# Cross attention with x1 turned and multiplied two pairs behind instead of three, w loaded and split earlier, the mask matmul of pair 0 last

## The chip, the cores and the metric

The kernel is one launch on one core of a Trainium2 chip. TensorE (PE) multiplies, VectorE (DVE), ScalarE (ACT) and GpSimd (POOL) do the elementwise work, SyncE (SP) and ACT issue the transfers. Each engine has its own stream of instructions and takes them in order; a semaphore holds an instruction until others have been counted. The metric is the device time of the launch in microseconds; smaller is better.

## The reference

Three blocks on x (32 sequences of 64 tokens, 512 wide), one after the other:

```
x = x + cross_attention(layernorm(x), ctx, mask)    # ctx: 32 x 256 x 512
x = x + latent_attention(layernorm(x), ...)         # 16 heads; q from 384, kv from 128 latent columns, rope on 64
x = x + ffn(layernorm(x), ...)                      # 512 -> 2048 -> 512, an expert term, a layernorm
```

Cross attention, with the latents that the next block needs, is what the change touches:

```
scores = einsum('bsd,bmd->bsm', hidden, memory) / sqrt(D);  scores = where(mask, scores, -1e30)
readout = einsum('bsm,bmd->bsd', softmax(scores), memory);  x1 = x + readout
q = rmsnorm(layernorm(x1) @ wq_a.T + b);  kv, k_pe = layernorm(x1) @ wkv_a.T + b   # kv normed, k_pe rotated
```

## The kernel before

`stage_x` handles the 2048 tokens as 16 pairs of sequences, 128 tokens each. Every engine runs `slot(p, par)` for p from 0 to 15; an order written out by hand in `slot` sets what stands behind what on each engine. In slot p the kernel works on several pairs at once:

- Pair p: `score(p)` on PE multiplies the turned, normalised x (`xnT0`) with the turned context (`ctxT`, ring of four) in eight matmuls (sixteen rows in the trace), onto the mask rows that a first matmul (`picks`) put there. DVE takes `maximum(p)`, ACT `exp(p)`, PE turns the probabilities into `b_prob`.
- Pair p+1: PE `turn0(p+1)` turns `xn0`; ACT `turned0(p+1)` copies it to `xnT0`.
- Pair p+2: DVE `first_var(p+2)` takes mean and variance; POOL `rstd_of(0, p+2)` makes rstd and shift; ACT `norm(0, ...)` applies them one slot later.
- Pair p-1: ACT `turned_probs` copies `b_prob` to `pT`; PE `read(p-1)` multiplies it with `ctx_in` (ring of four); DVE `residual(p-1)` adds it to x, which is x1, and takes its mean and variance; POOL `rstd_of(1, p-1)`, ACT `norm(1, ...)` to `xn1`.
- Pair p-2: PE `turn1` turns `xn1`, ACT `turned1_hi` copies it rounded, DVE `turned1_lo` takes the rest, so that three matmuls (hi and lo, `mm3`) make up a full one.
- Pair p-3: PE `project` multiplies it with the latent weights `w_hi`, `w_lo` (24 matmuls to `b_z`); DVE `bias` adds the bias to `zb`.
- Pair p-4: ACT `squares`, DVE `latent_var`, POOL `latent_rstd` and `rotate` (four steps), ACT `scale_q`, DVE `latent_kv`; `write_z` on ACT's queue stores the latents.

SP loads x, `ctxT`, `ctx_in`, and once `w_raw` (1152 KB) and `small`. `w_hi` is a cast of `w_raw`, `w_lo` a subtraction on DVE. After slot 15 the last pairs are drained by calls written out in `program`, between fills of the next block's weights (`fill_keys`, `keys_hi`, `keys_lo`, `fill_bias`; `rope_scaled` on POOL multiplies two blocks of 1536 columns). A reader should keep three waits in mind: `project(p)` waits for `xT1_lo`, `score(p)` for `xT0`, `norm(1, p)` for `shift1`.

Of the kernel before, what the change touches and what calls it, by code (L numbers as in the profile page):

```python
# [182 lines left out]
def stage_x(nc, ctx, A, scratch, mem, banks, w):  # L183
# [204 lines left out]
    def scalar(act):  # L388
# [42 lines left out]
        def slot(p, par):  # L431
# [4 lines left out]
            if has(p - 4):  # L436
                squares(p - 4, par)
            exp(p)
            if has(p - 4):
                scale_q(p - 4, par)  # L440
# [1672 lines left out]
```

## Time and profile before

| | us |
|---|---|
| Median of three runs (1086.8, 1087.6, 1095.32) | 1087.6 |
| Profiled execution, device time | 1087.94 |
| Its span, first to last instruction | 1086.1 |
| PE busy, share of the span | 1061.9, 98% |
| DVE, ACT, POOL busy | 509.6, 338.8, 295.5 |

The cross attention stage ends some 165 us into the span. A busy share tells how much an engine does, not whether it is waited for; the rows of the next sections are read for that. Starts and durations in a timeline are in microseconds from the span's start, an instruction's end may overlap the next one's start, and the bracket at a row's end says how long the engine was idle before it and who released it.

### The profile page before, as it was taken

What the parts mean: (1) busy time and instruction counts of PE and PEld (TensorE: products, weight loads), DVE (VectorE), ACT (ScalarE), POOL (GpSimd) and SP (SyncE); (2) the same over time, 40 slices, a digit from 0 to 9 for tenths busy, and PEclk for the clock granted to TensorE, in tenths of its full rate; (3) what the DMA queues carried; (4) which work ended last, traced back from release to release, by engine and by line L of the source; (5) the groups of instructions that cost most, each with busy time, mean ns of one, the idle gap of its engine ahead of it and who ended that gap; (6) DMA issues with size and microseconds to landing.
All of it is one profiled execution on the core that took longest, in us unless ns stands there. A gap on an engine that the chain in (4) does not pass through costs nothing.

```text
span 1086.1 us, 18670 instructions
## 1 busy us (share of the span) xinstructions
PE 1061.9 (98%) x7233; PEld 902.5 (83%) x7233; DVE 509.6 (47%) x914; ACT 338.8 (31%) x630; POOL 295.5 (27%) x341
## 2 busy tenths in 40 slices
PE   5999999999999999999999999999999999999997
PEld 3677787788888888888888889999999898989896
DVE  3666565545455554445545668532324241414232
ACT  3565554423222222222322236312222221313030
POOL 2434462311112101131113102423233232415050
PEclk9999999999999999999999999999999999999999
DMA  9999962200022000320012083200101010101000
GB/s 361 414 418 386 395 257 85 69 21 20 21 69 88 20 22 11 107 59 21 20 59 88 20 261 87 72 23 17 39 1 40 1 39 0 39 1 39 1 21 20
DMA packets 40851, 101.26 MB, mean 93 GB/s; under 512 B 7049, under 2 KB 11172, under 8 KB 36292
## 3 DMA queue, kind: packets, MB, share of 16 engines
q1 hardware_dynamic: 39044, 96.62, 25.0%
q10 hardware_dynamic: 1728, 3.54, 0.8%
q8 instruction: 55, 0.90, 0.3%
q14 instruction: 24, 0.20, 0.1%
HBM read 74.45 MB, written 17.30 MB: 84 GB/s over the span
## 4 chain that ended last, share of the span: by engine, by line
PE 94%; DVE 2%; issue 1%; DMA 1%; POOL 1%; ACT 0%; SPq 0%; POOLq 0%; DVEq 0%; ACTq 0%
PE b_z L44 6%; PE b_z L46 6%; PE b_z L45 6%; PE b_score L44 5%; PE b_score L46 5%; PE b_prob L46 5%; PE b_prob L44 5%; PE b_score L45 5%; PE b_prob L45 5%; PE b_turn L44 4%; PE b_turn L46 4%; PE b_turn L45 4%; PE b_read L46 4%; PE b_read L44 4%; PE b_read L45 4%; PE b_read L619 2%
## 5 line engine op out<-in xcount | busy, mean ns | idle before, releaser
L1501 POOL TENSOR_TENSOR f_hT_lo<-f_h,f_hT_hi 128x512 fp32r<-128x512 f32 x64 | 92.5, 1445 | 106.2 <-ACT f_hT_hi L1546 96.9
L810 POOL TENSOR_TENSOR m_sc<-m_sc,m_rs 128x1024 f32<-128x1024 f32 x16 | 30.6, 1910 | 241.8 <-DVE m_rs L973 241.8
L1602 DVE TENSOR_TENSOR f_h<-f_h 128x512 f32<-128x512 f32 x64 | 49.8, 777 | 91.7 <-ACT f_h L1541 91.7
L44 PE MATMUL b_z<-m_zT_lo,m_wq_hi 128*128 128x512 f32 x192 | 75.0, 390 | 0.9 <-issue 0.6
L46 PE MATMUL b_z<-m_zT_hi,m_wq_hi 128*128 128x512 f32 x192 | 74.7, 389 | 0.0
L45 PE MATMUL b_z<-m_zT_hi,m_wq_lo 128*128 128x512 f32 x192 | 74.7, 389 | 0.0
L44 PE MATMUL b_turn<-f_xnT_lo,f_up_hi 128*128 128x256 f32 x256 | 72.6, 283 | 0.1
L44 PE MATMUL b_read<-f_xnT_lo,f_up_hi 128*128 128x256 f32 x256 | 72.5, 283 | 0.0
L45 PE MATMUL b_read<-f_xnT_hi,f_up_lo 128*128 128x256 f32 x256 | 72.4, 283 | 0.0
L46 PE MATMUL b_turn<-f_xnT_hi,f_up_hi 128*128 128x256 f32 x256 | 72.4, 283 | 0.0
L45 PE MATMUL b_turn<-f_xnT_hi,f_up_lo 128*128 128x256 f32 x256 | 72.4, 283 | 0.0
L46 PE MATMUL b_read<-f_xnT_hi,f_up_hi 128*128 128x256 f32 x256 | 72.4, 283 | 0.0
L981 DVE TENSOR_TENSOR m_x<-b_score,m_x 128x512 f32<-128x512 f32 x32 | 22.1, 690 | 95.1 <-PE b_score L46 95.1
L852 ACT ACTIVATE m_qT<-b_z,m_q_bias 128x512 f32<-128x512 f32 x64 | 44.0, 689 | 70.4 <-PE b_z L46 64.6
L800 POOL TENSOR_TENSOR m_qpe<-m_qpe,m_swapped 128x512 f32<-128x512 f32 x32 | 41.4, 1292 | 79.0 <-DMA m_swapped<-m_by_sin 79.0
L1546 ACT CAST f_hT_hi<-f_h 128x512 fp32r<-128x512 f32 x64 | 39.8, 622 | 57.3 <-DVE f_h L1602 57.3
L1541 ACT ACTIVATE f_h<-b_turn 128x512 f32<-128x512 f32 x32 | 19.1, 598 | 112.8 <-PE b_turn L46 112.8
L1483 POOL TENSOR_TENSOR f_ve<-f_mv,m_eps 128x2 f32<-128x2 f32 x15 | 3.4, 227 | 182.3 <-DVE f_mv L1576 182.3
L873 ACT ACTIVATE m_sc<-m_sc 128x512 f32<-128x512 f32 x32 | 20.2, 632 | 104.8 <-DVE m_sc L965 104.8
L44 PE MATMUL b_score<-m_wvo_lo,m_oT_hi 128*128 128x512 f32 x128 | 51.4, 401 | 0.0
L44 PE MATMUL b_score<-f_down_lo,f_hT_hi 128*128 128x512 f32 x128 | 50.5, 394 | 0.3 <-issue 0.3
L44 PE MATMUL b_prob<-m_wvo_lo,m_oT_hi 128*128 128x512 f32 x128 | 50.6, 395 | 0.0
(268 smaller groups left out, 3098.6 us busy)
## 6 DMA issues: line engine op xcount, KB each, us to landing
x_ctx_in<-ctx_rows_dram SPq DMA_DIRECT2D x16, 1024.0 KB, 14.9
x_ctxT<-ctx_turned_dram SPq DMA_DIRECT2D x15, 1024.0 KB, 14.5
m_swapped<-m_by_sin SPq DMA_DIRECT2D x128, 64.0 KB, 2.0
m_raw<-attn_raw_dram SPq DMA_DIRECT2D x6, 768.0 KB, 10.9
m_z_in<-z_scratch SPq DMA_DIRECT2D x4, 1152.0 KB, 5.7
x_x_all<-x_dram SPq DMA_DIRECT2D x16, 256.0 KB, 15.1
m_x<-x_scratch SPq DMA_DIRECT2D x4, 1024.0 KB, 6.0
x_scratch<-m_x SPq DMA_DIRECT2D x4, 1024.0 KB, 5.1
```

Of the source, the lines that this page charges most:

```text
L44: nc.tensor.matmul(out, lh, rl, start=first, stop=False)
L45: nc.tensor.matmul(out, ll, rh, start=False, stop=False)
L46: return nc.tensor.matmul(out, lh, rh, start=False, stop=last)
L619: mm = t.matmul(b_read[rows], pT[:, c, rows], ctx_in[:, p % RING, chunks * b + c], start=c == 0, stop=c == chunks - 1)
L800: q.tensor_tensor(qpe[:, m], qpe[:, m], swapped[:], ALU.add).then_inc(s["qpe_done"], 1)
L810: q.tensor_tensor(e, e, rs[:].unsqueeze(2).broadcast_to([P, HB, SEQ]), ALU.mult).then_inc(s["normed"], 1)
L852: a.activation(qT[:, h], b_q[h % 2][:], ACT.Identity, bias=q_bias[:, HU * n + h:HU * n + h + 1]).then_inc(s["q_done"], 1)
L873: a.activation(sc[:, HALF * half:HALF * half + HALF], sc[:, HALF * half:HALF * half + HALF], ACT.Exp, scale=SCALE).then_inc(s["exped"], 1)
L981: v.tensor_tensor(x1[:, TILES[i]], b_w[i % 2][:], x1[:, TILES[i]], ALU.add).then_inc(s["x2_done"], 1)
L1501: g.tensor_tensor(hT_lo[:, 2 * n:2 * n + 2].rearrange("p m n -> p (m n)"), h[:, n % 2], hT_hi[:, 2 * n:2 * n + 2].bitcast(F32).rearrange(" ...
L1546: a.copy(hT_hi[:, 2 * n:2 * n + 2].rearrange("p m n -> p (m n)"), h[:, n % 2]).then_inc(s["h_hi"], 1)
L1602: v.tensor_tensor(h[:, n % 2], h[:, n % 2], h[:, n % 2], ALU.mult).then_inc(s["squared"], 1)
```

## The change

The order of the slots moves: on every engine the work that stood at p-3 (project, bias) is now at p-2 and that at p-4 at p-3. On TensorE, turn1(p-2) moves ahead of read(p-1), in slot 2 even ahead of score(2), with project(0) behind score(2). On ACT the hi copy moves ahead of exp, on DVE the lo copy ahead of first_var. The cast to `w_hi` moves from POOL in slot 2 to ACT in slot 1, ahead of norm(1, 0); w is loaded ahead of ctxT(2). 22 transposes of the identity precede turn0(0). The mask matmul of pair 0 comes last in its group. `rope_scaled` moves from behind slot 15 into slots 14 and 15, first on POOL. The drain in `program` is one pair shorter.

```
+    WARM = 22
 (sync)
+        load_ctxT(1)
         load_x(2)
-        load_ctxT(1)
         load_ctx(0)
         load_x(3)
+        sp.dma_start(w_raw[:], ...).then_inc(s["w_loaded"], 16)
         load_ctxT(2)
+        load_x(4)
         load_ctx(1)
-        load_x(4)
-        sp.dma_start(w_raw[:], ...).then_inc(s["w_loaded"], 16)
+        sp.dma_start(small[:], A["small"]).then_inc(s["small_loaded"], 16)
         load_ctxT(3)
 (gpsimd slot)
+            if p >= PAIRS - w.ROPE_ROUNDS:
+                rope_scaled(p - (PAIRS - w.ROPE_ROUNDS))
             if has(p + 2):
                 rstd_of(0, p + 2)
-            if has(p - 4):
-                latent_rstd(p - 4)
-                rotate(p - 4, par)
+            if has(p - 3):
+                latent_rstd(p - 3)
+                rotate(p - 3, 1 - par)
             if has(p - 1):
                 rstd_of(1, p - 1)
-            if p == 2:
-                pool.wait_ge(s["w_loaded"], 16)
-                g.tensor_copy(w_hi[:], w_raw[:]).then_inc(s["w_hi"], 1)
 (scalar slot)
+            if has(p - 3):
+                squares(p - 3, 1 - par)
             if has(p - 2):
                 turned1_hi(p - 2, par)
+            exp(p)
+            if has(p - 3):
+                scale_q(p - 3, 1 - par)
             if has(p + 1):
                 turned0(p + 1)
+            if p == 1:
+                act.wait_ge(s["w_loaded"], 16)
+                a.copy(w_hi[:]..., w_raw[:]...).then_inc(s["w_hi"], 1)
             if has(p - 1):
                 norm(1, p - 1, xn1, x_all[:, p - 1])
 (vector slot)
             maximum(p)
+            if has(p - 2):
+                turned1_lo(p - 2, par)
             if has(p + 2):
                 first_var(p + 2)
...
             validate(p)
-            if has(p - 3):
-                bias(p - 3, 1 - par)
+            if has(p - 3):
+                latent_kv(p - 3, 1 - par)
+            if has(p - 2):
+                bias(p - 2, par)
 (tensor slot)
+            if p == 2:
+                turn1(p - 2)
             score(p)
+            if p == 2:
+                project(p - 2, par)
+            if p > 2:
+                turn1(p - 2)
             if has(p - 1):
                 read(p - 1)
-            if has(p - 2):
-                turn1(p - 2)
             if has(p + 1):
                 turn0(p + 1)
-            if has(p - 3):
-                project(p - 3, 1 - par)
+            if p > 2:
+                project(p - 2, par)
 (program, tensor, after slot 15)
-            x["turn1"](L - 1)
-            x["project"](L - 2, L % 2)
-            x["read"](L)
-            w["fill_keys"](0)
+            w["fill_keys"](0)
+            x["read"](L)
+            x["turn1"](L - 1)
             w["fill_keys"](1)
+            w["fill_keys"](2)
             x["project"](L - 1, 1 - L % 2)
-            w["fill_keys"](2)
             x["turn1"](L)
             w["fill_keys"](3)
+            w["fill_keys"](4)
             x["project"](L, L % 2)
-            w["fill_keys"](4)
```

TensorE, one pair in the middle, before. `b_prob` is the turned probabilities, `x_picks` and `x_ctxT` the score, `x_xn_108` turn1, `x_xn_104` turn0; 24 matmuls to `b_z` (project) follow each.

```order
L568 MATMUL b_prob<-m_ident,x_probs 128x128 [waits x_pT,x_exped]
L568 MATMUL b_prob<-m_ident,x_probs 128x128
L601 MATMUL b_score<-x_picks 128x256 [waits x_ctxT_loaded0,x_exped,x_xT0]
L607 MATMUL b_score<-x_ctxT,x_xnT_105 64x256 x8
L619 MATMUL b_read<-x_ctx_in,x_pT 64x512 [waits x_x1_done,x_ctx_loaded3,x_pT]
L619 MATMUL b_read<-x_ctx_in,x_pT 64x512 x3
L568 MATMUL b_turn<-m_ident,x_xn_108 128x128 [waits x_xT1_lo,x_norm1]
L568 MATMUL b_turn<-m_ident,x_xn_108 128x128 x3
L568 MATMUL b_turn<-m_ident,x_xn_104 128x128 [waits x_xT0,x_norm0]
L568 MATMUL b_turn<-m_ident,x_xn_104 128x128 x3
L44 MATMUL b_z<-x_w_lo,x_xnT1b_hi 128x288 [waits x_z_biased,x_xT1_lo]
```

The same place after the change:

```order
L571 MATMUL b_prob<-m_ident,x_probs 128x128 [waits x_pT,x_exped]
L571 MATMUL b_prob<-m_ident,x_probs 128x128
L603 MATMUL b_score<-x_picks 128x256 [waits x_ctxT_loaded3,x_exped,x_xT0]
L609 MATMUL b_score<-x_ctxT,x_xnT_105 64x256 x8
L571 MATMUL b_turn<-m_ident,x_xn_108 128x128 [waits x_xT1_lo,x_norm1]
L571 MATMUL b_turn<-m_ident,x_xn_108 128x128 x3
L624 MATMUL b_read<-x_ctx_in,x_pT 64x512 [waits x_x1_done,x_ctx_loaded2,x_pT]
L624 MATMUL b_read<-x_ctx_in,x_pT 64x512 x3
L571 MATMUL b_turn<-m_ident,x_xn_104 128x128 [waits x_xT0,x_norm0]
L571 MATMUL b_turn<-m_ident,x_xn_104 128x128 x3
L44 MATMUL b_z<-x_w_lo,x_xnT1b_hi 128x288 [waits x_z_biased,x_xT1_lo]
```

turn1 has moved from behind read to ahead of it, and the project that follows is that of the same x1.

ACT, from norm(1, ...) of one slot to the next hi copy (`x_xnT1.._hi`), before. `x_pT` is turned_probs, `x_junk` the squares, `x_probs` exp, `x_zbuf` scale_q.

```order
L395 ACTIVATE x_xn_108<-x_x_all,x_shift_127,x_rstd_125 128x512 [waits x_turned1,x_shift1]
L258 DMA z_scratch<-x_zbuf 128x576 [waits x_q_scaled,x_z_rope,x_z_kv]
L417 COPY x_pT<-b_prob 128x256 [waits x_read,x_p_turned]
L395 ACTIVATE x_xn_104<-x_x_all,x_shift_126,x_rstd_124 128x512 [waits x_turned0,x_shift0]
L422 ACTIVATE x_junk,x_ssq<-x_zb 128x384 [waits x_q_var,x_z_biased]
L424 ACTIVATE x_junk,x_ssq<-x_zb 128x128 [waits x_squared]
L412 ACTIVATE x_probs,x_esum<-b_score,x_negmax 128x256 [waits x_validated,x_p_turned,x_maxed]
L429 ACTIVATE x_zbuf<-x_zb,x_q_rstd 128x384 [waits x_z_stored1,x_q_rstd]
L406 CAST x_xnT1b_hi<-b_turn 128x512 [waits x_z_made,x_turned1]
L400 COPY x_xnT_105<-b_turn 128x512 [waits x_scored,x_turned0]
```

And after:

```order
L395 ACTIVATE x_xn_108<-x_x_all,x_shift_127,x_rstd_125 128x512 [waits x_turned1,x_shift1]
L259 DMA z_scratch<-x_zbuf 128x576 [waits x_q_scaled,x_z_rope,x_z_kv]
L417 COPY x_pT<-b_prob 128x256 [waits x_read,x_p_turned]
L395 ACTIVATE x_xn_104<-x_x_all,x_shift_126,x_rstd_124 128x512 [waits x_turned0,x_shift0]
L422 ACTIVATE x_junk,x_ssq<-x_zb 128x384 [waits x_q_var,x_z_biased]
L424 ACTIVATE x_junk,x_ssq<-x_zb 128x128 [waits x_squared]
L406 CAST x_xnT1a_hi<-b_turn 128x512 [waits x_z_made,x_turned1]
L412 ACTIVATE x_probs,x_esum<-b_score,x_negmax 128x256 [waits x_validated,x_p_turned,x_maxed]
L429 ACTIVATE x_zbuf<-x_zb,x_q_rstd 128x384 [waits x_z_stored1,x_q_rstd]
L400 COPY x_xnT_105<-b_turn 128x512 [waits x_scored,x_turned0]
```

The hi copy has moved from behind exp and scale_q to directly behind the squares.

DVE, from maximum(p) to the lo copy (`x_xnT1.._lo`), before; `x_stats_118` belongs to first_var, `x_stats_119` to residual.

```order
L503 TENSOR_REDUCE x_negmax<-b_score 128x1 [waits x_validated,x_scored]
L467 BN_STATS x_stats_118<-x_x_all 128x6 [waits x_x_loaded4]
L471 BN_AGGR x_mean_var_120<-x_stats_118 128x2 [waits x_stats0,x_shift0,x_x_loaded0]
L474 TENSOR_SCALAR x_var_eps_122<-x_mean_var_120 128x1 [waits x_var0]
L486 TENSOR_SCALAR x_q_var<-x_ssq 128x1 [waits x_squared,x_q_rstd]
L486 TENSOR_SCALAR x_q_var<-x_ssq 128x1
L517 SCALAR_TENSOR_TENSOR x_x_all<-b_read,x_rvalid,x_x_all 128x512 [waits x_validated,x_read]
L467 BN_STATS x_stats_119<-x_x_all 128x6 [waits x_x1_done,x_x_loaded0]
L471 BN_AGGR x_mean_var_121<-x_stats_119 128x2 [waits x_stats1,x_shift1,x_x_loaded0]
L476 TENSOR_SCALAR x_var_eps_123<-x_mean_var_121 128x1 [waits x_var1]
L462 TENSOR_TENSOR x_xnT1a_lo<-b_turn,x_xnT1a_hi 128x512 [waits x_z_made,x_xT1_hi]
```

And after, up to the statistics of residual:

```order
L506 TENSOR_REDUCE x_negmax<-b_score 128x1 [waits x_validated,x_scored]
L465 TENSOR_TENSOR x_xnT1a_lo<-b_turn,x_xnT1a_hi 128x512 [waits x_z_made,x_xT1_hi]
L470 BN_STATS x_stats_118<-x_x_all 128x6 [waits x_x_loaded4]
L474 BN_AGGR x_mean_var_120<-x_stats_118 128x2 [waits x_stats0,x_shift0,x_x_loaded0]
L477 TENSOR_SCALAR x_var_eps_122<-x_mean_var_120 128x1 [waits x_var0]
L489 TENSOR_SCALAR x_q_var<-x_ssq 128x1 [waits x_squared,x_q_rstd]
L489 TENSOR_SCALAR x_q_var<-x_ssq 128x1
L520 SCALAR_TENSOR_TENSOR x_x_all<-b_read,x_rvalid,x_x_all 128x512 [waits x_validated,x_read]
L470 BN_STATS x_stats_119<-x_x_all 128x6 [waits x_x1_done,x_x_loaded0]
```

The lo copy has moved from behind residual to ahead of first_var.

## Rows read from the trace of the kernel before

**Rows 1.** The waits of TensorE, whole span: for what, us in total, times, longest.
```profile
PE b_turn L568 <- ACT x_xn L395: 7.4, 2, 7.1
PE b_score L601 <- DVE x_picks L557: 2.3, 1, 2.3
PE b_z L1300 <- DVE x_zb L531: 1.2, 1, 1.2
```

**Rows 2.** TensorE's timeline: start us, us, engine, line, operation, tiles.
```profile
10.73 3.54 PE L607 MATMUL b_score<-x_ctxT,x_xnT 128*64 128x256 f32 x16
37.78 1.95 PE L607 MATMUL b_score<-x_ctxT,x_xnT 128*64 128x256 f32 x16
46.58 1.95 PE L607 MATMUL b_score<-x_ctxT,x_xnT 128*64 128x256 f32 x16
```

**Rows 3.** The window 10 to 20 us: busy us of PE, PEld, DVE, ACT, POOL; granted clock, DMA, GB/s.
```profile
10.00:20.00 10.00, 8.99 (x51) 4.49 (x52) 3.44 (x12) 3.32 (x8) 1.03 (x3) 1.00 1.01 412
```

**Rows 4.** One steady pair as a window, columns as in rows 3.
```profile
78.86:86.98 8.12, 8.12 (x62) 5.95 (x59) 5.22 (x17) 4.84 (x13) 3.29 (x9) 1.00 1.03 423
```

**Rows 5.** The transfer of w: its issue, its size and us to landing; POOL's cast.
```profile
7.48 0.43 SPq L323 DMA_DIRECT2D x_w_raw<-w_latent_dram  x1
x_w_raw<-w_latent_dram SPq DMA_DIRECT2D x1, 1152.0 KB, 17.3
29.31 2.10 POOL L381 CAST x_w_hi<-x_w_raw 128x2304 fp32r<-128x2304 f32 x1
```

**Rows 6.** From residual on DVE to norm1 on ACT, pair 1.
```profile
26.16 0.75 DVE L517 SCALAR_TENSOR_TENSOR x_x_all<-b_read,x_rvalid,x_x_all 128x512 f32<-128x512 f32 x1 [1.41 <-PE b_read L619]
29.40 0.81 ACT L395 ACTIVATE x_xn<-x_x_all,x_shift,x_rstd 128x512 f32<-128x512 f32 x1 [1.60 <-POOL x_shift L351]
```

**Rows 7.** ACT's timeline in and around that steady pair.
```profile
78.45 0.82 ACT L395 ACTIVATE x_xn<-x_x_all,x_shift,x_rstd 128x512 f32<-128x512 f32 x1 [0.55 <-POOL x_shift L351]
79.17 0.35 ACT L417 COPY x_pT<-b_prob 128x256 f32<-128x256 f32 x1
79.43 0.81 ACT L395 ACTIVATE x_xn<-x_x_all,x_shift,x_rstd 128x512 f32<-128x512 f32 x1
80.14 0.51 ACT L422 ACTIVATE x_junk<-x_zb 128x384 f32<-128x384 f32 x1
84.97 0.57 ACT L406 CAST x_xnT1b_hi<-b_turn 128x512 fp32r<-128x512 f32 x1
86.57 0.82 ACT L395 ACTIVATE x_xn<-x_x_all,x_shift,x_rstd 128x512 f32<-128x512 f32 x1 [0.55 <-POOL x_shift L351]
```

**Rows 8.** The same steady pair on DVE, and its first row on POOL.
```profile
81.39 0.69 DVE L467 BATCH_NORM_STATS2 x_stats<-x_x_all 128x6 f32<-128x512 f32 x1
85.57 0.69 DVE L462 TENSOR_TENSOR x_xnT1b_lo<-b_turn,x_xnT1b_hi 128x512 fp32r<-128x512 f32 x1 [0.75 <-ACT x_xnT1b_hi L406]
86.17 0.15 DVE L507 RECIPROCAL x_rinv<-x_esum 128x1 f32<-128x1 f32 x1
82.76 0.55 POOL L347 TENSOR_TENSOR x_rstd<-x_var_eps,m_neg_half 128x1 f32<-128x1 f32 x1 [4.34 <-DVE x_var_eps L474]
```

**Rows 9.** ACT's timeline late in the stage, the squares and a hi copy behind them.
```profile
136.12 0.52 ACT L422 ACTIVATE x_junk<-x_zb 128x384 f32<-128x384 f32 x1
137.08 0.56 ACT L406 CAST x_xnT1a_hi<-b_turn 128x512 fp32r<-128x512 f32 x1
```

**Rows 10.** POOL's rope_scaled, both.
```profile
135.97 5.46 POOL L1355 TENSOR_TENSOR m_raw<-m_raw,m_vec_cols 128x1536 f32<-128x1536 f32 x2
```

**Rows 11.** DVE and POOL side by side, at two places.
```profile
156.83 3.44 POOL L1364 TENSOR_TENSOR m_wq_lo<-m_raw,m_wq_hi 128x1536 fp32r<-128x1536 f32 x1
156.90 3.52 DVE L491 SCALAR_TENSOR_TENSOR x_zbuf<-x_zb,x_q_rstd,x_small 128x128 f32<-128x128 f32 x1
45.18 0.35 DVE L491 SCALAR_TENSOR_TENSOR x_zbuf<-x_zb,x_q_rstd,x_small 128x128 f32<-128x128 f32 x1
45.47 0.27 POOL L351 TENSOR_SCALAR x_shift<-x_mean_var,x_rstd 128x1 f32<-128x1 f32 x1 [0.53 <-POOL x_rstd L347]
```

More of the change, by code:

```diff
@@ L326, in sync, with gpsimd @@
         load_x(5)
-        sp.dma_start(small[:], A["small"]).then_inc(s["small_loaded"], 16)
         slots(slot)
         return dict(store_z=store_z, store_x1=store_x1)
-    def gpsimd(pool):
+    def gpsimd(pool, rope_scaled):
         g = nc.gpsimd
@@ L435, in slot @@
                 norm(0, p + 1, xn0, x_all[:, p + 1])
[L436 to L440, printed above, removed]
+            if has(p - 3):
+                squares(p - 3, 1 - par)
             if has(p - 2):
                 turned1_hi(p - 2, par)
+            exp(p)
+            if has(p - 3):
+                scale_q(p - 3, 1 - par)
             if has(p + 1):
                 turned0(p + 1)
+            if p == 1:
+                act.wait_ge(s["w_loaded"], 16)
+                a.copy(w_hi[:].rearrange(flat), w_raw[:].rearrange(flat)).then_inc(s["w_hi"], 1)
             if has(p - 1):
                 norm(1, p - 1, xn1, x_all[:, p - 1])
-            if has(p - 4):
-                write_z(act, p - 4, par)
+            if has(p - 3):
+                write_z(act, p - 3, 1 - par)
         norm(0, 0, xn0, x_all[:, 0])
@@ L607, in score @@
                     mm = t.matmul(b_score[rows, 0:CTX], xnT0[:, k, rows], ctxT[:, p % RING, k, CTX * b:CTX * b + CTX],
-                                  start=False, stop=k == KH - 1)
+                                  start=p == 0 and k == 0, stop=p != 0 and k == KH - 1)
+            if p == 0:
+                pe.wait_ge(s["masks_built"], 1)
+                mm = t.matmul(b_score[:, 0:CTX], picks[:, p].bitcast(BF16), mask_rows, start=False, stop=True)
             mm.then_inc(s["scored"], 1)
@@ L639, in tensor @@
         pe.wait_ge(s["consts"], 3)
+        for n in range(WARM):
+            t.transpose(banks.free[:, P * (n % 4):P * (n % 4) + P], ident[:], ident[:])
         turn0(0)
@@ L1776, in _ @@
         def _(pool):
-            x, w = X["gpsimd"](pool), weights.gpsimd(pool)
-            m = M["gpsimd"](pool)
-            for n in range(weights.ROPE_ROUNDS):
-                w["rope_scaled"](n)
-            x["latent_rstd"](L - 3)
-            x["rotate"](L - 3, 1 - L % 2)
+            w = weights.gpsimd(pool)
+            x, m = X["gpsimd"](pool, w["rope_scaled"]), M["gpsimd"](pool)
             x["rstd_of"](1, L)
@@ L1876, in _ @@
             x, w, m = X["vector"](dve), weights.vector(dve), M["vector"](dve)
-            x["latent_var"](L - 3)
+            x["residual"](L)
             x["turned1_lo"](L - 1, 1 - L % 2)
-            x["latent_kv"](L - 3, 1 - L % 2)
-            x["bias"](L - 2, L % 2)
-            x["residual"](L)
+            x["latent_var"](L - 2)
             w["keys_lo"](0)
+            x["latent_kv"](L - 2, L % 2)
             w["keys_lo"](1)
+            w["keys_lo"](2)
             x["bias"](L - 1, 1 - L % 2)
-            x["latent_var"](L - 2)
             x["turned1_lo"](L, L % 2)
-            x["latent_kv"](L - 2, L % 2)
-            w["keys_lo"](2)
+            x["latent_var"](L - 1)
             w["keys_lo"](3)
             w["keys_lo"](4)
-            x["latent_var"](L - 1)
+            x["latent_kv"](L - 1, 1 - L % 2)
             x["bias"](L, L % 2)
-            x["latent_kv"](L - 1, 1 - L % 2)
-            for f in range(5, 9):
+            for f in range(5, 7):
                 w["keys_lo"](f)
             x["latent_var"](L)
-            w["keys_lo"](9)
+            for f in range(7, 9):
+                w["keys_lo"](f)
             x["latent_kv"](L, L % 2)
-            for f in range(10, weights.KEY_FILLS):
+            for f in range(9, weights.KEY_FILLS):
                 w["keys_lo"](f)
```

39 lines of the change are left out of this document (17 added, 22 removed).

## The prediction

> **What bounds the kernel now.** I read the waits of TensorE first, then TensorE's timeline from the start, then one pair in the middle of cross attention on all engines. The waits of TensorE are short everywhere: the longest are the 7.1 us until the first normalised tile (the 7.4 us row), 2.3 us for the mask rows of pair 0, and 1.2 us for a bias late in the stage [rows 1]. So TensorE's stream is the path almost from end to end. Whatever it loses in this stage, the end loses, unless a later wait shrinks by as much, and the later waits are too small for that. A gain can come only out of waits, since the change removes no matmul: every pair still scores, reads, turns and multiplies.
>
> At the start, the sixteen score matmuls of pair 0 take 3.54 us, those of pair 4 take 1.95 us [rows 2]. That is another 1.6 us lost at the start, although the granted clock of 10 to 20 us is given as 1.00 [rows 3]; before them the engine had run four transposes only. In the same stretch the DMA engines are full, at 412 GB/s [rows 3].
>
> From pair 5 on a pair takes 8.12 us, and TensorE is busy for all of it; DVE is busy 5.22 us, ACT 4.84, POOL 3.29 [rows 4]. These shares look roomy. They are no proof that the other engines can follow: each of them works in order, and a chain that goes from one to the next and comes back one pair later has a period of its own. That is what I price below.
>
> **The change, part by part. (1) The start.** With the mask matmul last, score(0) no longer waits for the mask rows from 8.8 to 10.4 us but only for xnT0 and for the second half of ctxT; with the 22 transposes ahead, its matmuls should run at the pace of pair 4. Together some 3.6 us earlier: 2.0 to 2.3 of mask wait and 1.6 of pace, against the end of score(0) at 14.3. The transposes themselves lie in the 7.1 us in which TensorE waits anyway: 22 at the slow pace of 3.54 us for sixteen are 4.9 us.
>
> The Trainium skill, "TensorE: Matmul & The Clock Gate", section "Part 1: The HAM clock gate", says that the default state is throttled and that matmul activity releases it. The two paces in the rows agree, the granted clock column does not show it. By the rule alone the warm-up would be worth its 1.6 us at the end of the kernel; by the next paragraph it is worth nothing there.
>
> What becomes of the 3.6 us? The next things TensorE needs come by DMA at the same pace as before, and one of them has been put in front of pair 0's x1: ACT now copies w_hi in slot 1, ahead of norm1(0). The w transfer is issued at 7.48 us and lands 17.3 us later, at 24.8 [rows 5]. x4, ctxT(2) and ctx(1) go behind it: 2304 KB, 2.36 MB, at 412 GB/s 5.7 us. So w lands at 19.1 us. POOL's cast of it took 2.10 us [rows 5]; ACT needs about the same, until 21.2. norm1(0) takes 0.81, so turn1(0), which now stands **ahead of** score(2), starts at 22.1, whatever score(0) gained. I follow TensorE from there: turn1(0) to 22.5, score(2) to 24.5 (its ctxT, behind w, lands at about 21.6), then project(0), which waits for the hi and lo copies (the lo stands behind maximum(2) on DVE: 24.7 + 0.35 + 0.7) until 25.8, to 29.1; read(1) to 30.9; turn0(3) and the turned probabilities to 31.6. The copy of xnT0(3), 0.59 us, lets score(3) start at 32.3 and end at 34.2. turn1(1) waits for norm1(1): read(1) is seen at 31.05, from residual to norm1 it takes 3.24 us [rows 6], with 0.81 for norm1 that is 35.1, a wait of 0.9. read(2) and turn0(4) run to 37.8; ACT meanwhile goes norm1(1) 34.3, then 2.65 us to the hi copy (steps in part 2) 36.95, the lo copy is done at 38.25, project(1) runs to 41.55. score(4) then waits for xnT0(4), which on ACT stands behind the scaling of q: first_var(5) at 38.15, 1.37 to POOL, 1.65 for rstd, shift and q_rstd, 0.52 and 0.6 on ACT: 42.35. So the sixteen matmuls of score(4) start at 42.55, before at 37.78 [rows 2]: 4.8 us later, of which project(1), 3.26 us, was done ahead of its old place. One slot on I expect 51.6 against 46.58 [rows 2], 5.0 later, 3.26 of it work done ahead: **the start costs 1.7 us net**. Bounds: w one us earlier or later moves it by one us, so 0 to 3.
>
> **(2) The steady pairs.** In the old order ACT copied x1's hi part after exp and scale_q, and DVE the lo part after residual. Now the hi copy of pair p-2 stands ahead of exp(p), and the lo copy ahead of first_var(p+2). Take the start of the hi copy as zero and follow who waits for whom, with spacings from start to start:
> - hi copy on ACT to lo copy on DVE: 84.97 to 85.57, 0.60 [rows 7, 8].
> - lo copy to the next instruction of DVE, now first_var: 85.57 to 86.17, 0.60 [rows 8].
> - first_var(p+2) on DVE to rstd0 on POOL: 81.39 to 82.76, 1.37 [rows 8]. POOL works in order: rstd0, shift0, q_rstd, four rope steps, rstd1, shift1.
> - rstd0 on POOL to norm1(p-1) on ACT: 82.76 to 86.57, 3.81 [rows 7, 8].
> - norm1 to the copy of pT: 78.45 to 79.17, 0.72; pT to norm0: 0.26; norm0 to the squares: 0.71 [rows 7].
> - squares to the hi copy, which now follows them directly: 136.12 to 137.08, 0.96 [rows 9].
>
> That is the hi copy of the next pair, and the sum is **9.03 us**. Nothing in this circle waits for TensorE, so no spare time of TensorE shortens it: a pair cannot take less than 9.03 us, where it takes 8.12. In the old order the circle was open: first_var stood behind maximum only, which waits for score, and the hi copy stood behind it, so POOL could start on pair p+2 right after score(p). The 0.91 us shows as waits of TensorE for the lo copy (ahead of project) and for xnT0 (ahead of score). Slots 5 to 13, nine intervals from score(5) to score(14), give 9 x 0.91 = **8.2 us**. Bounds: zero if some link is not a link; upwards see the rival on the shared read interface.
>
> **(3) The end of the stage.** Slots 14 and 15 have no first_var, which opens the circle, but POOL gets rope_scaled ahead of rstd1: two of them took 5.46 us [rows 10], 2.7 each. With first_var POOL's rstd0 and shift0 are gone too, and POOL was busy 3.29 of 8.12 us, so most of it should find room; I take **0.4 us** for both slots, nearer to 0 than to the other bound, one of them on the path in full, 2.7. In the tail, fill 4 now stands ahead of project(15), so DVE no longer holds bias(15) behind keys_lo(4), and the 1.2 us wait of the fill that needs the bias [rows 1] should go: **-1.2 us**, bounds -1.2 and 0. The SP order matters for w only; small lands earlier than needed either way, and the ring of ctxT and ctx refills with each score and read as before.
>
> **Sum.** The profiled execution took 1087.94 us (span 1086.1, 1.8 around it), 0.3 above the median of 1087.6. 1087.94 + 1.7 + 8.2 + 0.4 - 1.2 = **1097.0 us**.
>
> **The rivals. Another 3 us from DVE and POOL getting in each other's way (slower).** latent_kv on DVE reads two SBUF tiles. Where it ran beside POOL's 3.44 us subtraction, it took 3.52 us instead of 0.35; and where it ran at 45.18, POOL's shift started 0.53 us after rstd ended, not 0.17 [rows 11]. In the old steady pair it falls behind POOL's last step. In the new circle it falls at 4.85 to 5.20, amid POOL's rope steps (4.2 to 5.4), and those are on the circle. If each pair loses the 0.36 us, ten pairs lose 3.6: 1100.6 us. It decides from about 0.15 us per pair whether the time passes 1098.5. For it: the two places. Against: DVE may be the one that is held, as in the first of them, and latent_kv is not on the circle. 20%.
>
> The Trainium skill, "GPSIMD Engine Reference", in its table of specs, says that GpSimd's SBUF interfaces are shared with VectorE, with contention for instructions with two SBUF inputs. The 3.52 us row agrees.
>
> **The circle does not bind.** If ACT or POOL turn out to be ahead by more than the trace lets me see, a pair stays at 8.12 us, and the sum is 1087.94 + 1.7 - 1.2 + 0.4 = 1088.8. Against it: every link is a wait or an order of one engine, and each spacing is taken where the two stood back to back. 11%.
>
> **The change works as meant.** The 3.6 us of the start stay gained, since w lands early enough or norm1(0) isn't held by it, and the tail gives its 1.2: 1083.1 us. Against it: 19.1 us for w by bytes, and the place of the copy on ACT. 8%.
>
> **How the numbers follow.** My own case has 56%, with 1095 to 1099.5 as its range (0.75 to 1.05 us lost per pair, 1 to 2.5 at the start). 5% are left for something above 1102, rope_scaled on the path in full among it. The range 1091 to 1102 holds my case, the slower rival and the near side of what is between; it leaves out the two cheap cases, 19%. About 1% is what a measurement can tell from no change: 1098.5 and 1076.7. Above 1098.5 lie a quarter of my own case, most of the 20% and the 5%, together 0.37. Below 1076.7 would need more than all of the waits at the start, 0.01. The rest, 0.62, is within 1%.
>
> **What would show it.** In the profile after: score(0) done by about 10.7 us; ACT's w_hi at about 19.1, norm1(0) at about 21.2, turn1(0) at 22.1; the spacing of scores in the middle 9.0 us, with waits of TensorE of 0.3 and 0.6 us per pair, released by the lo copy and by xnT0; no other engine much busier than before. Wrong would be: a spacing of 8.12; scores 9.4 apart (the slower rival); a wait for turn1(0) much shorter than 4 us.

## The result and the profile after

The changed kernel takes 1098.5 us (median of 11 runs, 1097.18 to 1100.95). The kernel before, run beside it, takes 1092.74 (11 runs, 1086.76 to 1095.39). The ratio is 1.006, with a 95% interval of 1.0039 to 1.0081: slower, by less than 1%. The two profiled executions stand at 1098.49 and 1087.94 us, spans 1096.7 and 1086.1, so between the traces lie 10.6 us, between the medians only 5.8. Both gaps have to be explained. One run of the kernel before that stood beside experiments 1 to 4 (1520.32 us at a mean granted clock of 0.655) was a slow one and is left out of every figure below.

**Where the 10.6 us lie.** TensorE's timeline of the changed kernel, at the start of the stage (columns as in rows 2):

```profile
8.10 1.95 PE L609 MATMUL b_score<-x_ctxT,x_xnT 128*64 128x256 f32 x16 [0.67 <-ACT x_xnT L400]
20.90 1.12 PE L571 MATMUL b_turn<-m_ident,x_xn 128*128 128x128 f32 x4 [3.75 <-ACT x_xn L395]
22.16 3.68 PE L609 MATMUL b_score<-x_ctxT,x_xnT 128*64 128x256 f32 x16
44.22 1.95 PE L609 MATMUL b_score<-x_ctxT,x_xnT 128*64 128x256 f32 x16
53.22 1.95 PE L609 MATMUL b_score<-x_ctxT,x_xnT 128*64 128x256 f32 x16
```

score(0) starts at 8.10 us and takes 1.95, where it started at 10.73 and took 3.54 [rows 2]. Then TensorE waits 3.75 us for the first norm1 tile, and score(2) runs at the slow pace, 3.68 us for sixteen matmuls. score(5) starts at 53.22 against 46.58 [rows 2], with one project (3.26 us) done ahead of its old place: 6.64 - 3.26 = **3.4 us** lost. Up to score(14) the changed kernel needs 81.16 us (53.22 to 134.38), before 73.36 (46.58 to 119.94): **7.8 us**. score(14) to score(15) takes 8.42 against 8.11: **0.3 us**. From score(15) to the first transposition of the next stage it is 40.16 against 44.36, of which one project fewer makes 3.26: **-0.9 us**. That is 10.6 together; from there on both kernels take 913.7 us.

score(14), score(15) and the first transposition of the next stage, of the changed kernel and then of the kernel before:

```profile
134.38 1.95 PE L609 MATMUL b_score<-x_ctxT,x_xnT 128*64 128x256 f32 x16
142.80 1.95 PE L609 MATMUL b_score<-x_ctxT,x_xnT 128*64 128x256 f32 x16
182.96 0.49 PE L1051 MATMUL b_turn<-m_ident,m_z_in 128*128 128x128 f32 x3
```
```profile
119.94 1.95 PE L607 MATMUL b_score<-x_ctxT,x_xnT 128*64 128x256 f32 x16
128.05 1.95 PE L607 MATMUL b_score<-x_ctxT,x_xnT 128*64 128x256 f32 x16
172.41 0.49 PE L1040 MATMUL b_turn<-m_ident,m_z_in 128*128 128x128 f32 x3
```

**The waits of TensorE** in the changed kernel, as in rows 1:

```profile
PE b_turn L571 <- ACT x_xn L395: 5.4, 4, 3.8
PE b_score L603 <- ACT x_xnT L400: 5.0, 12, 0.8
PE b_z L1311 <- DVE x_zb L534: 0.4, 1, 0.4
```

The 2.3 us for the mask rows are gone, the 1.2 us for the bias are 0.4 [rows 1], and xnT0 is waited for in twelve slots. In a steady pair it is the only wait of TensorE that the view shows; the forecast one for the lo copy isn't there.

**The clock at the start.** Windows of the changed kernel, columns as in rows 3:

```profile
15.00:20.00 5.00, 2.14 (x14) 0.84 (x9) 3.04 (x9) 3.06 (x5) 1.62 (x4) 0.93 1.04 408
20.00:22.00 2.00, 1.10 (x5) 0.85 (x5) 1.84 (x1) 1.82 (x4) 0.00 (x0) 0.50 1.05 431
22.00:24.00 2.00, 2.00 (x12) 1.07 (x12) 0.72 (x1) 0.58 (x1) 0.00 (x0) 0.50 1.03 416
24.00:26.00 2.00, 1.84 (x10) 0.62 (x6) 0.12 (x1) 0.00 (x0) 0.00 (x0) 0.50 1.01 411
26.00:30.00 4.00, 3.04 (x23) 3.04 (x24) 1.84 (x5) 0.56 (x2) 0.81 (x2) 0.99 1.01 409
```

The granted clock falls inside the 3.75 us wait, at about 19.3 us by the 0.93 of the first window, and is 0.50, the 1.2 GHz level, until about 26 us; 5 us of TensorE's work lie in that stretch. What held norm1(0) is seen on ACT, and w comes with 12.4 us from issue to landing, not 17.3 [rows 5]:

```profile
18.02 2.11 ACT L447 CAST x_w_hi<-x_w_raw 128x2304 fp32r<-128x2304 f32 x1 [0.47 <-DMA x_w_raw<-w_latent_dram]
20.04 0.81 ACT L395 ACTIVATE x_xn<-x_x_all,x_shift,x_rstd 128x512 f32<-128x512 f32 x1
```

**A steady pair.** ACT, then DVE and POOL, in the pair that answers to rows 7 and 8:

```profile
83.69 0.56 ACT L406 CAST x_xnT1a_hi<-b_turn 128x512 fp32r<-128x512 f32 x1
90.05 0.81 ACT L395 ACTIVATE x_xn<-x_x_all,x_shift,x_rstd 128x512 f32<-128x512 f32 x1 [1.03 <-POOL x_shift L352]
90.77 0.35 ACT L417 COPY x_pT<-b_prob 128x256 f32<-128x256 f32 x1
91.03 0.81 ACT L395 ACTIVATE x_xn<-x_x_all,x_shift,x_rstd 128x512 f32<-128x512 f32 x1
91.74 0.51 ACT L422 ACTIVATE x_junk<-x_zb 128x384 f32<-128x384 f32 x1
92.69 0.57 ACT L406 CAST x_xnT1b_hi<-b_turn 128x512 fp32r<-128x512 f32 x1
84.29 0.69 DVE L465 TENSOR_TENSOR x_xnT1a_lo<-b_turn,x_xnT1a_hi 128x512 fp32r<-128x512 f32 x1 [1.67 <-ACT x_xnT1a_hi L406]
84.89 0.68 DVE L470 BATCH_NORM_STATS2 x_stats<-x_x_all 128x6 f32<-128x512 f32 x1
86.25 0.55 POOL L348 TENSOR_TENSOR x_rstd<-x_var_eps,m_neg_half 128x1 f32<-128x1 f32 x1 [5.23 <-DVE x_var_eps L477]
```

Go round: hi copy 83.69, lo copy 84.29, first_var 84.89, rstd0 86.25, norm1 90.05, pT 90.77, norm0 91.03, squares 91.74, hi copy 92.69. That is 9.00 us, and it is the period of the scores (8.99 to 9.11 in the nine intervals from score(5) to score(14), 9.02 on average). No engine is much busier than in rows 4. The same pair as a window, from score(8) to score(9), one of the two longest intervals:

```profile
80.20:89.29 9.09, 8.70 (x60) 5.90 (x60) 5.39 (x18) 4.72 (x12) 3.38 (x10) 1.00 0.78 262
```

### The profile page after: what moved, and what is told of

Same layout as the page of the kernel before. It is cut to its first block, busy times and chain, and to the rows that moved or that the text cites. A ratio compares the mean times of both kernels' runs of the same rounds, so it can differ in the third digit from the quotient of the medians.

```text
span 1096.7 us, 18715 instructions
## 1 busy us (share of the span) xinstructions
PE 1072.7 (98%) x7255; PEld 906.8 (83%) x7255; DVE 507.5 (46%) x914; ACT 339.4 (31%) x631; POOL 292.4 (27%) x340
## 4 chain that ended last, share of the span: by engine, by line
PE 85%; DVE 3%; POOL 3%; ACT 3%; issue 2%; DMA 2%; ACTq 0%; SPq 0%; POOLq 0%; DVEq 0%
PE b_score L44 5%; PE b_score L46 5%; PE b_z L44 5%; PE b_prob L46 5%; PE b_prob L44 5%; PE b_score L45 5%; PE b_prob L45 5%; PE b_z L45 5%; PE b_z L46 5%; PE b_turn L44 4%; PE b_turn L46 4%; PE b_turn L45 4%; PE b_read L46 4%; PE b_read L44 4%; PE b_read L45 4%
## 5 line engine op out<-in xcount | busy, mean ns | idle before, releaser
L992 DVE TENSOR_TENSOR m_x<-b_score,m_x 128x512 f32<-128x512 f32 x32 | 22.1, 690 | 94.6 <-PE b_score L46 94.6
L1552 ACT ACTIVATE f_h<-b_turn 128x512 f32<-128x512 f32 x32 | 19.1, 598 | 112.3 <-PE b_turn L46 112.3
```

What stands on the lines that cost most here:

```text
L992: v.tensor_tensor(x1[:, TILES[i]], b_w[i % 2][:], x1[:, TILES[i]], ALU.add).then_inc(s["x2_done"], 1)
L1552: a.activation(h[:, n % 2], bank_u(i, n)[:], ACT.Relu).then_inc(s["relu"], 1)
```

## The experiments

Three questions: does the circle set the 9.0 us; what does the start cost, and why; and what lies behind the gap between the medians. Ratios are to the kernel before, run beside each experiment on the same chip. The changed kernel was not run again beside them, so a difference to its 1098.5 us goes between two sets of runs; the faster runs of the kernel before lay from 1086.6 to 1088.5 us in every set.

**1. The hi copy ahead of the squares.**
```diff
+            if has(p - 2):
+                turned1_hi(p - 2, par)
             if has(p - 3):
                 squares(p - 3, 1 - par)
-            if has(p - 2):
-                turned1_hi(p - 2, par)
```


> The changed kernel with one step moved on ACT: the hi copy of pair p-2 ahead of the squares of pair p-3 instead of behind them. Theory (the circle sets the pace): this takes the 0.96 us of the squares off the circle, 9.03 - 0.96 = 8.07 us, below the 8.12 us that TensorE needs, so scores come 8.12 us apart in the middle and the time falls by the 7.8 us that pairs 5 to 14 lost, to 1090.5 us. Rival (something other than the circle, such as DVE or POOL being held by each other, costs the pairs their 0.9 us): the spacing stays at 9.0 and the time at 1098.5.

Measured: 1092.91 us (1091.28 to 1094.65), ratio 1.0027 (1.0003 to 1.005). The circle was the limit: 5.6 us came back, by one step of ACT moved. Between the profiled executions it is 6.7: 5.0 from score(5) to score(14), 2.0 ahead of score(5), and 0.5 lost from score(14) to score(15). But in the middle scores stand 8.43 us apart, not 8.12, and TensorE has no wait in between. The same step in two kernels shows what is longer. First the kernel before, then this one; TensorE's timeline from score to the first product with w:

```profile
79.06 1.95 PE L607 MATMUL b_score<-x_ctxT,x_xnT 128*64 128x256 f32 x16
80.84 1.89 PE L619 MATMUL b_read<-x_ctx_in,x_pT 128*64 128x512 f32 x8
82.65 1.09 PE L568 MATMUL b_turn<-m_ident,x_xn 128*128 128x128 f32 x8
83.50 0.38 PE L44 MATMUL b_z<-x_w_lo,x_xnT1a_hi 128*128 128x288 f32 x1
```
```profile
84.90 1.95 PE L609 MATMUL b_score<-x_ctxT,x_xnT 128*64 128x256 f32 x16
86.78 0.66 PE L571 MATMUL b_turn<-m_ident,x_xn 128*128 128x128 f32 x4
87.36 1.94 PE L624 MATMUL b_read<-x_ctx_in,x_pT 128*64 128x512 f32 x8
89.23 0.66 PE L571 MATMUL b_turn<-m_ident,x_xn 128*128 128x128 f32 x4
89.65 0.38 PE L44 MATMUL b_z<-x_w_lo,x_xnT1b_hi 128*128 128x288 f32 x1
```

Before: 1.78 from score to read, 1.81 to the eight transposes, 0.85 to the product. Here: 1.88 to turn1, 0.58, 1.87, 0.42. The sum is 4.44 before and 4.75 here: 0.31 us for a place of turn1 between score and read.

**2. first_var ahead of the lo copy.**
```diff
+            if has(p + 2):
+                first_var(p + 2)
             if has(p - 2):
                 turned1_lo(p - 2, par)
-            if has(p + 2):
-                first_var(p + 2)
```


> The changed kernel with one step moved on DVE: first_var(p+2) ahead of the lo copy of pair p-2, so first_var no longer waits for the hi copy. Theory (the circle): opened at this link, spacing 8.12 us in the middle. In slots 2 and 3 the lo copy comes some 1.4 us later and with it project, which costs about 0.7 to 1.1 us once: 1098.5 - 7.8 + 0.9 = 1091.6 us. Rival (the order on ACT alone is what costs, whoever stands behind first_var): 9.0 us apart, 1098.5 or more.

Measured: 1095.06 us (1092.38 to 1097.09), ratio 1.0019 (0.9997 to 1.0042). Cut at another link, the circle opens just as well: 8.43 us apart. The start costs more than expected. The wait for the lo copy of pair 0 is 2.23 us instead of 1.12, the clock stays below 1.00 until beyond 30 us (0.84 from 26 to 30, 0.89 from 30 to 40), and score(3) comes at 36.05, 2.3 us later than in the changed kernel.

**3. The wait at the start filled.**
```diff
             if p == 2:
+                for n in range(32):
+                    t.transpose(banks.free[:, P * (n % 4):P * (n % 4) + P], ident[:], ident[:])
                 turn1(p - 2)
```


> The changed kernel with 32 transposes of the identity into the free bank in the 3.75 us in which TensorE waits for the first norm1 tile. Theory (the wait let TensorE's clock fall to 0.50, and score(2) and what follows ran at the slow pace): the granted clock stays at 1.00 from 18 to 26 us, the sixteen matmuls of score(2) take 1.95 us, not 3.68, and everything behind is 1.6 us earlier: 1096.9 us. Rival (project(0) waits for w_lo or the lo copy anyway, or score(2)'s slowness has another cause, such as its operands being written by DMA): no change, 1098.5, with score(2) either at 3.7 us or at 1.95 us and a wait behind it.

Measured: 1097.02 us (1096.2 to 1097.76), ratio 1.0046 (1.0025 to 1.0067). TensorE's timeline of this kernel, and two of its windows:

```profile
17.34 3.66 PE L631 MATMUL b_free<-m_ident 128*128 128x128 f32 x32
21.25 0.66 PE L571 MATMUL b_turn<-m_ident,x_xn 128*128 128x128 f32 x4 [0.26 <-ACT x_xn L395]
21.95 1.95 PE L609 MATMUL b_score<-x_ctxT,x_xnT 128*64 128x256 f32 x16
```
```profile
20.00:22.00 2.00, 1.75 (x17) 1.30 (x15) 1.49 (x1) 2.00 (x4) 0.00 (x0) 1.00 1.06 429
22.00:24.00 2.00, 1.89 (x17) 1.00 (x16) 1.13 (x2) 0.64 (x2) 0.00 (x0) 1.00 1.01 409
```

turn1(0) starts no earlier (21.25), yet the clock stays at 1.00, score(2) takes 1.95 us, and score(3) comes 2.0 us earlier. The results of the added transposes are never used; what they give is the pace. The runs also lie closer together, within 1.6 us instead of 3.8, with a mean granted clock of 0.998 or 0.999 in each. The Trainium skill, "TensorE: Matmul & The Clock Gate", section "Part 4: PE-mode transpose", says that transposes don't count as activity for the full clock in the way other work does; by it nothing would change here. The trace disagrees: 32 transposes and nothing else kept the clock at 1.00.

**4. No warm-up.**
```diff
-    WARM = 22
+    WARM = 0
```


> The changed kernel without the 22 transposes at the start. Theory (turn1(0) is held by the w transfer and ACT's copy of it, so what is gained in score(0) dies there): score(0) takes 3.5 us instead of 1.95, its end is 1.6 us later, turn1(0) stays at 20.9 us and the time at 1098.5. Rival (the warm-up is worth its pace at the end too): 1100.1 us.

Measured: 1099.41 us (1097.72 to 1100.99), ratio 1.0065 (1.0041 to 1.009), 0.9 us above the changed kernel, between the two theories. 0.9 us is little beside a spread of 3.3 in the runs; the trace shows where it comes from. score(0) takes 3.68 us, and ACT comes to the cast of w at 19.19, no longer in time for the transfer that landed at about 18.0. With the warm-up ACT had waited 0.47 us for w, so that much of the gain was slack, and the rest, about 1.2 us, reaches ACT's cast; score(2) is 0.8 us later without it.

**5. The kernel before once more.** No edit.

> The kernel before, unchanged, for a second look: its runs lie between 1087 and 1095 us, and the profiled one (1087.94) is at the low end. Theory: the runs differ in how long TensorE's clock stays low, which the warm-up and the waits at the start decide; a run of about 1094 us should show granted clocks below 1.00 in some stretch where the first profile has 1.00. Rival: the clock is the same and DMA or the end of the kernel differs. If this run comes out near 1087 us it tells nothing new.

Measured: 1094.27 us. Up to score(15) this run is no slower than the first profile (126.57 against 128.05 us). In the tail it loses 7.7 us: 52.09 us from score(15) to the next stage against 44.36. The wait for the bias, and the windows behind it:

```profile
155.44 0.83 PE L1300 MATMUL b_z<-m_vec_cols,m_raw 128*128 128x1 f32 x6 [1.18 <-DVE x_zb L531]
178.66 0.49 PE L1040 MATMUL b_turn<-m_ident,m_z_in 128*128 128x128 f32 x3
```
```profile
155.00:156.00 1.00, 0.56 (x5) 0.56 (x6) 0.96 (x3) 0.57 (x2) 1.00 (x2) 1.00 0.77 217
156.00:157.00 1.00, 1.00 (x9) 1.00 (x9) 1.00 (x1) 1.00 (x3) 1.00 (x1) 0.77 0.03 6
160.00:165.00 5.00, 5.00 (x25) 5.00 (x25) 2.27 (x6) 2.69 (x7) 1.98 (x3) 0.50 0.17 62
172.00:174.00 2.00, 2.00 (x4) 0.73 (x4) 0.69 (x1) 0.88 (x2) 0.00 (x0) 0.60 0.80 193
```

From about 156.5 to 173.6 us the granted clock is 0.50, though TensorE has no further wait there; ahead of it stand the 1.18 us wait and matmuls one column wide. The 1087.94 us execution has the same two waits (0.51 us for the last lo copy, 1.18 us for the bias) and 1.00 throughout. So the theory was right on the clock and wrong on the place: it is the tail, not the start.

**6. The kernel before, with the warm-up alone.** The 22 transposes of the change, ahead of turn0(0).

> The kernel before with the 22 transposes ahead of the first turn and nothing else. Theory (the start's slow pace is what makes the runs of before differ): score(0) takes 1.95 us, the runs lie within 2 us of each other, at 1087 us, since project(0) waits for w_lo until 34.1 us in any case and takes the 1.6 us gained back. Rival (the clock is lost elsewhere in the kernel): the runs still lie between 1087 and 1095 us with a median of about 1093.

Measured: 1090.68 us, five runs from 1086.34 to 1087.88 and five from 1093.47 to 1096.59, ratio 1.0001 (0.9968 to 1.0034). The rival held, as 5 lets one expect, and in the faster group nothing is gained. The theory also had the pace of score(0) wrong:

```profile
10.30 0.27 PE L601 MATMUL b_score<-x_picks 128*128 128x256 bf16 x1 [2.81 <-DVE x_picks L557]
10.50 3.62 PE L607 MATMUL b_score<-x_ctxT,x_xnT 128*64 128x256 f32 x16
```

Between the warm-up and score(0) lies the 2.81 us wait for the mask rows, and the granted clock is 0.50 from about 10.5 to 13.9 us. The 22 transposes give score(0) its pace only together with the mask moved last, where its wait is 0.67 us.

**7. The kernel before, with the change's start.** Warm-up, pair 0's mask last, SyncE's order; the pipeline and the cast of w as before.

> The kernel before with the change's start and nothing of the shorter pipeline: 22 transposes, pair 0's mask last, and SyncE's order of the change (w ahead of ctxT(2)); w_hi stays POOL's in slot 2, so norm1(0) is not held. Theory: score(1) starts 3.9 us earlier than the 16.09 us of before, nothing takes it back since w_lo is there before project(0), and the time is 1084 us. Rival (DMA at 412 GB/s or another wait at the start takes it back): 1087.

Measured: 1096.73 us, one run at 1087.2 and nine from 1095.97 to 1098.03, ratio 1.0032 (1.0002 to 1.0061). score(1) starts at 12.16, 3.9 us earlier, as expected; score(2) then waits 3.47 us for ctxT(2), which stands behind w, and behind that wait the clock is 0.50 from 22.0 to 25.4 us, so that score(2) takes 3.23 us. Nothing of the gain reaches the end, and score(5) comes 0.7 us later than before. The profiled run is one of the nine slower ones, and it loses its time in the tail again (52.06 us, with 0.50 from about 158.5 to 175.6 us).

**8. The kernel before, with turn1 ahead of read.**
```diff
+            if has(p - 2):
+                turn1(p - 2)
             if has(p - 1):
                 read(p - 1)
-            if has(p - 2):
-                turn1(p - 2)
```


> The kernel before with turn1(p-2) ahead of read(p-1) on TensorE, as in the changed kernel, and nothing else. The runs so far show pairs of 8.42 us with TensorE without a wait in the new order against 8.12 us in the old. Theory (going from score's matmuls to transposes and back to read's costs TensorE itself about 0.3 us, which score followed by read does not): scores 8.42 us apart here too, 13 or 14 pairs, 4.2 us slower than before at the same clock. Rival (the 0.3 us come from other engines' new order, such as contention or a wait too short for the trace): 8.12 us apart and no change.

Measured: 1091.07 us, eight runs from 1090.16 to 1091.76 and two at 1098.26 and 1099.03, ratio 1.0009 (0.9978 to 1.004). A steady pair:

```profile
79.17:87.59 8.42, 8.42 (x60) 5.84 (x59) 5.31 (x17) 4.83 (x13) 3.46 (x9) 1.00 1.02 418
```

8.42 us with TensorE busy throughout. The eight faster runs have a median of 1091.0, 3.9 us more than the 1087.1 of the nine faster runs of the kernel before beside them; 4.2 was expected. The 0.3 us belong to TensorE's order, whatever the other engines do.

**9. The kernel before, with the fill of keys 4 ahead of project(15).**
```diff
+            w["fill_keys"](4)
             x["project"](L, L % 2)
-            w["fill_keys"](4)
```


> The kernel before with one step moved on TensorE in the tail: the fill of keys 4 ahead of project(15), as the changed kernel has it. In a run of before of 1094.27 us the clock fell to 0.50 from about 157 us for some 16 us, just behind the 1.18 us wait for bias(15); in the 1087.94 us run, with the same waits, it stayed at 1.00. Theory (that wait is what lets the clock fall in most runs of before, and its removal is what keeps the changed kernel from it): the wait shrinks to about 0.4 us, all runs lie at 1087 us, none above 1089, so the median falls by 6 us. Rival (the 0.51 us wait for the lo copy and the narrow matmuls of the bias are enough, or it is something later in the kernel): still two groups, 1087 and 1094, median above 1090.

Measured: **1084.26 us, all eight runs from 1083.89 to 1084.99**, ratio 0.9942 (0.9917 to 0.9966). Better than expected: not only the bias wait is gone, but also the 0.51 us for the last lo copy and 0.36 us for a fill. So the edit takes away three waits (2.05 us) at once, and doesn't tell which of them lets the clock fall. From score(15) to the next stage it takes 41.65 us instead of 44.36. One window of the tail, where 5 had 0.50:

```profile
160.00:165.00 5.00, 5.00 (x30) 3.57 (x29) 4.43 (x7) 3.05 (x5) 4.86 (x7) 1.00 0.16 62
```

**10. That, with the warm-up and pair 0's mask last.** SyncE's order as before.

> The kernel before with the fill of keys 4 ahead of project(15), the 22 transposes and pair 0's mask last, SyncE's order left as before. Theory: score(1) at 12.2 us instead of 16.1, ctxT(2) comes in time with this order (with w ahead of it score(2) waited 3.5 us), and TensorE meets its next limit at project(0), which waits for w_lo; POOL's cast of w can start when w lands at 24.8 us, 4.5 us earlier than now, if slot 2 is earlier by as much. Then 2 to 3 us are gained: 1084 to 1085 us in all runs. Rival (w_lo or the DMA pace takes it back): 1087.

Measured: 1083.91 us (seven runs, 1082.86 to 1085.3), ratio 0.9928 (0.9902 to 0.9954). Within the spread of 9, so the start gives nothing that can be told from zero. score(2) starts 2.9 us earlier than in the first profile; then score(3) waits 3.87 us for ctxT(3), which SyncE's queue has behind w, and the clock drops after it (0.50 from about 29 to 32 us). The rival's mechanism held: the transfers take it back. Its 1087 us, like the theory's gain of 2 to 3 us, was counted from a kernel at 1087, before 9 had shown 1084.3.

**11. The changed kernel with both mends (1 and 3).**

> The changed kernel with both mends: the hi copy ahead of the squares and 32 transposes in the wait for turn1(0). Theory: the two add up, pairs of 8.43 us and no clock lost at the start, 1089.9 us, all runs within 2 us. Rival (the two overlap): 1091.3, the fastest of the kernel with the hi copy ahead alone.

Measured: 1090.88 us (1089.86 to 1091.88), ratio 0.9997 (0.9973 to 1.002). They add up: 7.6 us below the changed kernel, where the two gave 5.6 and 1.5 apart; the half us over is within the spread of the runs. One row is new, at score(15):

```profile
135.26 0.28 PE L603 MATMUL b_score<-x_picks 128*128 128x256 bf16 x1 [0.89 <-ACT x_xnT L400]
```

score(14) to score(15) takes 9.50 us here, not 8.43: the copy to xnT0 stands behind ACT's scaling of q, this waits 3.59 us for q_rstd, and q_rstd stands on POOL behind rope_scaled, which waits 4.48 us for its own load. In the changed kernel score(14) is 8.4 us later, that wait is 1.48 us, and none of it is seen on TensorE.

**12. The changed kernel with the fill of keys 4 behind project(15),** the reverse of the edit in 9.

> The changed kernel with one step put back in the tail: the fill of keys 4 behind project(15), as before the change. Moving it forward in the kernel before took its runs from 1087 to 1095 us down to 1083.9 to 1085.0. Theory (the place of this fill alone decides whether TensorE waits for bias(15) and whether the clock falls there): the wait of about 1.2 us returns, the fastest runs are 1 to 3 us slower than the changed kernel's 1097.2, and more than half of the runs lose a further 6 to 8 us, up to 1106, with a mean granted clock near 0.99. Rival (the rest of the changed tail, with its other order on ACT and DVE, protects it too): one group of runs, 1098 to 1101 us.

Measured: 1102.65 us, four runs from 1101.36 to 1102.79 and two at 1106.17 and 1107.47, ratio 1.0146 (1.012 to 1.0173).

```profile
170.04 0.83 PE L1311 MATMUL b_z<-m_vec_cols,m_raw 128*128 128x1 f32 x6 [0.83 <-DVE x_zb L534]
```

The wait for the bias is 0.83 us (0.41 in the changed kernel, 1.18 before), 0.51 us for the last lo copy is back, and the tail takes 41.60 us instead of 40.16. A second group appears, in two of six runs, not in more than half. The profiled run is one of the four others: its clock is 1.00 in the tail, so that the two slower ones fell there is likely (mean granted clock 0.990 and 0.992) and not shown. The fastest lies 4.2 us above the changed kernel's fastest, more than the 1 to 3 expected; of the 2.9 us between the profiled executions 0.9 lie ahead of score(15) and 1.4 in the tail. So the place of the fill matters in this kernel too. Whether the rest of the changed tail protects it in part, six runs can't tell.

## Why the prediction came out as it did

Right were the sign, the time to 1.5 us and the main mechanism. Term by term:

- **Steady pairs: 8.2 forecast, 7.8 measured.** The circle is there with all its links, 9.00 us for the 9.03 worked out, and it set the pace (1 and 2). The waits of TensorE were 0.4 us per pair, not 0.9, all for xnT0. This is because the step "a pair ... where it takes 8.12" was wrong for the new order: TensorE alone needs 8.43 us once turn1 stands between score and read (8). (Of the 0.57 us between 8.43 and 9.00 the waits show 0.39; the rest is overlap between the turned probabilities and the mask matmul, which follows them after 0.77 us here and after 0.21 in experiment 1.) It changed nothing in this sum, since the circle was longer still. But the rivals "the circle does not bind" (1088.8) and "the change works as meant" (1083.1) were both priced some 3 us too low by it: 0.31 us over nine to eleven pairs. The diff showed that place of turn1, and no row of before shows this change of tiles in a steady pair.
- **Start: 1.7 forecast, 3.4 measured.** w landed at 18.0 instead of 19.1, ACT's copy of it did hold norm1(0), and turn1(0) came at 20.90, earlier than the 22.1 of the text. The failed step is the next: "turn1(0) to 22.5, score(2) to 24.5" took the full pace for granted behind a wait that the text itself had put at 4 us. The clock had fallen to 0.50; with the wait filled (3) score(5) starts at 51.27, and the term is 51.27 - 46.58 - 3.26 = 1.4. The clock cost 2.0 us; by the text's own rule (w one us earlier moves the start by one us) the early turn1(0) should have made the term 0.5, so two errors of opposite sign met in it.
- **Slots 14 and 15: 0.4 forecast, 0.3 measured, by luck.** 8.42 us from score(14) to score(15) is the new order's own period (8.43), so the 0.3 us are again the place of turn1, which the forecast had left out, and POOL's two rope_scaled, 2.75 us each, cost nothing there. With the circle opened the slots come earlier, the first of them starts late behind its load, and TensorE loses 1.1 us (11).
- **The tail: -1.2 forecast, -0.9 measured** between the two profiles. As a statement on the medians it is far too small (below).
- **DVE and POOL in each other's way (20%)** did not happen. latent_kv ran beside one of POOL's rope steps:

```profile
88.40 0.37 DVE L494 SCALAR_TENSOR_TENSOR x_zbuf<-x_zb,x_q_rstd,x_small 128x128 f32<-128x128 f32 x1
88.37 0.25 POOL L367 TENSOR_TENSOR x_rope_tmp<-x_zb,x_small 128x32 f32<-128x32 f32 x1
```

The four rope steps took 0.32, 0.26, 0.25 and 0.32 us, as in the kernel before, where latent_kv falls behind them. The 3.52 us row [rows 11] remains the one case of a long wait, beside a 3.44 us POOL operation.
- **A reading of the rows.** The mask wait of pair 0 goes from 8.15 to 10.43 us, not from 8.8 to 10.4; its 2.28 us, which the sum of the start uses, are right.

**The gap of the medians.** The prediction took 1087.94 us as the kernel's time. That is the lower of two levels: in each set of its runs, a part lies at 1087 and another at 1090.6 to 1095.6, with a mean granted clock of 0.998 in the one and 0.990 to 0.994 in the other. The 1095.32 among the three runs in the table of times was a sign of it that the prediction passed over. By 5 the difference is the clock in the tail, by 9 it is gone when the fill of keys 4 stands ahead of project(15). The changed kernel has that order, and none of its 11 runs, nor of the 49 of experiments 1 to 4 and 11, is more than 4.8 us above the fastest of its kernel, where the kernels with the old order (before, 6 to 8) spread by 7 to 11. What spread is left in them lies mostly at the start: with the wait filled it is 1.6 us (3) and 2.0 us (11). So the change lost 10.6 us, and got about half of it back where before loses its clock. How large that half is depends on how many runs of before fall: 8 of 11 beside the changed kernel, 3 of 11 beside experiment 12. That 1097.0 came so near 1098.5 is in part luck: the changed kernel's runs show no slower level, and the base happened to be an execution without it. From the 1095.32 us run the same terms would have given 1104.4, outside the range.

Open is why one execution falls and the next with the same waits does not, and which of the waits in the tail it hangs on (9 took three away at once). Why TensorE needs 0.31 us more with turn1 between score and read is located in the timeline, not explained.

## What to carry to other kernels

A pipeline made shorter must be walked round once for each pair of engines that now wait for each other within one iteration: add the spacings from start to start until you are back, and compare with the bottleneck engine's own period in the *new* order. Here moving one copy ahead of one squaring gave back 5.6 us, about what the whole change had lost by the medians. A wait on TensorE costs more than its length wherever the clock may fall behind it, and a kernel whose runs lie in two groups should be looked at in both before a base is taken; the best version here is the kernel before with one fill moved, 1084.3 us (1083.9 with the warm-up and pair 0's mask last, which is not to be told from it).
